# A six-block decoder on one core: projections and normalisations fused by chunks, expert choice inside the expert loop, head attention in fours

## The chip, the core and the metric

One core of a Trainium2 chip runs the whole program. TensorE (PE, its weight loads PEld) multiplies, VectorE (DVE), ScalarE (ACT) and GpSimd (POOL) work on vectors, SyncE (SP) issues DMAs; each runs its own queue in order, and they wait for each other's semaphores. The metric is the device time in microseconds (us), the median of three executions.

## The reference

`x` holds 32 sequences of 56 tokens with 128 features (1792 tokens); the context holds 32 × 1500 × 128 numbers. Every block is "add to x what a sublayer makes of the layer-normalised x":

```python
x = x + retention(norm(x))                 # 16 heads of 8, decay, rms, silu gate, Wo
x = x + context_attention(norm(x), ctx)    # one head, softmax over 1500 keys, Wv
x = x + experts0(norm(x))                  # 8 experts of 512, top 2, relu(g) * u
x = x + causal_attention(norm(x))          # 16 heads, rotary, wo
x = x + head_attention(norm(x), ctx)       # 16 heads of 8 over 1500 keys, Wo, bo
x = x + experts1(norm(x))                  # 8 experts, top 2 with a capacity,
                                           # silu, + 0.1 * a shared expert
# top 2: p = softmax(logits); one-hot of the best and the second best;
# weights p1, p2 divided by their sum; experts1 also counts, by a running sum over
# tokens, who still fits an expert's capacity, and drops the others
```

## The kernel before

The stream `xt` lies transposed in SBUF, 128 features by 1792 tokens, and is worked in `CH` = 4 chunks of `CW` = 448. Each stage is one or more blocks of hand-written queues for the five engines; at a block's end all engines meet. Semaphores are wrapped in `Flow` objects, and `rolled` and `staged` repeat a slot in hardware loops.

Between two stages stand separate blocks. `project_back` multiplies the sublayer's output by its last matrix and adds it to `xt`. `normalize` centres each chunk by a matmul, squares it on ACT, averages by a matmul, takes `Ln` and `Exp`, and multiplies on DVE into `xn`. The next stage's first projections are a block again. The chain of a chunk crosses PE, ACT and DVE.

`choose` is one more block before each expert stage. PE makes 14 tiles of 128 × 8 logits; ACT copies `xh` (`xn` rounded to a shorter float) while POOL subtracts to get the remainder `xl` and rounds the first expert's weights (`ahead.high`, `ahead.low`). DVE finds best and second best in a chain of small steps (with `capacity`, also the running counts of both ranks, one after the other). PE transposes the weights in 14 small transposes, ACT copies them, a DMA writes them to DRAM. Every expert then reads its row of weights back, spread over 128 partitions, into `cb`.

`experts_relu` (experts0) and `experts_silu` (experts1) run units of one chunk by 128 hidden features, 16 to an expert. PE multiplies the unit up in pieces (high × high, low × high, high × low), ACT applies the activation, POOL rounds the hidden values (`hf` to `hh`), DVE subtracts (`hl`), and PE multiplies down some units later. `weigh` (DVE) multiplies a finished chunk by `cb` into `ow`, which is then added to `xt`: on POOL in experts0, on DVE in experts1. In experts1 nine experts run, the shared one last.

`head_attention` works in slots, each with three samples in flight: the keys of sample p, the maxima (`peak`, 21 matmuls with a DVE maximum over each) and values (`values`) of p−1, and the scores, exponentials and weighted values of p−2 over 12 tiles of 125 keys (`score`, ACT `Exp`, `weigh`). A slot has six parts:

```python
    IT = ST // 2
    PLACES = [(0, 1, 2, 3), (1, 2, 3), (0, 1, 2, 3), (1, 2, 3), (0, 1, 2, 3), (0, 1, 2)]
                        if sums and i >= 1:
                            weigh(p - 2, u, 2 * i - 2)
                            weigh(p - 2, u, 2 * i - 1)
```

After the last slot the projection runs in the same block, and then `normalize` as "n6".

## Time and profile before

| what | us |
|---|---|
| median of 3 executions (lowest, highest) | 1730.73 (1729.13, 1732.51) |
| the profiled execution, its own time | 1733.57 |
| its span, first to last instruction | 1731.8 |

| stretch of the profiled execution | us |
|---|---|
| begin, retention, to the first context score | 0 to 137.4 |
| context attention | 137.4 to 292.9 |
| projection, n3, choose | 292.9 to 331.2 |
| experts0 | 331.2 to 573.95 |
| n4, rotary, causal attention | 573.95 to 699.1 |
| projection, n5, prologue of head attention | 699.1 to 729.1 |
| head attention's slots | 729.1 to 1480 |
| projection, n6, choose | 1480 to 1531.9 |
| experts1 and the output | 1531.9 to 1731.8 |

PE is busy 1575.7 us of the span (91%), DVE 1179.3 (68%), ACT 877.7 (51%), POOL 656.6 (38%); the mean granted clock of TensorE is 0.952 of full speed. A busy share is a mean over all stages; the windows of a single stage tell what bounds it.

### The profile page before, as it was taken

The page shows a single profiled execution, that of the slowest core. Times are in us where ns is not written, and L with a number is a line of the kernel's source. Part 1 is how long each engine was busy: PE and PEld are TensorE (multiplying, and loading weights), DVE is VectorE, ACT ScalarE, POOL GpSimd, SP SyncE. Part 2 cuts the span into 40 slices and gives each one's busy share as a digit, 9 for nine tenths or more (in the row PEclk, how much of TensorE's full clock was granted, in tenths as well). Part 3 has the DMA queues.
Part 4 walks back from the last instruction along what each step waited for, and adds up shares of the span by engine and source line. Part 5 has one row for each costly group of instructions (what it writes and reads, how often), then busy time and mean ns, then how long its engine had stood idle before and what let it go on. Part 6 is the DMA issues. An engine that isn't in the chain of part 4 may idle for free. (4 is left out here: it accounts for less than half of the span.)

```text
span 1731.8 us, 45100 instructions
## 1 busy us (share of the span) xinstructions
PE 1575.7 (91%) x16384; PEld 1202.0 (69%) x16384; DVE 1179.3 (68%) x1863; ACT 877.7 (51%) x1337; POOL 656.6 (38%) x717
## 2 busy tenths in 40 slices
PE   7988998699999866689999999999999999759998
PEld 3535665599999555367777777777777777448887
DVE  3643554487887567567777777777777776359998
ACT  4463332232322345356666666666666666334443
POOL 0300000387877245232333333323333331138886
PEclk8998999699999979899999999999999999769999
DMA  2028991311110000366665555556655554022221
GB/s 72 1 56 227 258 263 53 99 40 53 66 39 22 0 2 1 89 156 143 143 142 132 127 128 127 127 139 142 142 135 126 128 128 88 13 69 68 67 67 43
DMA packets 53038, 169.76 MB, mean 98 GB/s; under 512 B 12593, under 2 KB 24497, under 8 KB 52962
## 3 DMA queue, kind: packets, MB, share of 16 engines
q1 hardware_dynamic: 50802, 157.22, 36.2%
q10 hardware_dynamic: 2160, 11.52, 2.2%
q8 instruction: 48, 0.79, 0.2%
q14 instruction: 28, 0.23, 0.0%
HBM read 91.18 MB, written 1.04 MB: 53 GB/s over the span
## 5 line engine op out<-in xcount | busy, mean ns | idle before, releaser
L1728 DVE TENSOR_REDUCE hat_tops<-banks 128x1 f32<-128x500 f32 x672 | 448.3, 677 | 138.9 <-PE banks L1524 138.7
L1632 ACT ACTIVATE hat_pb<-banks 125x896 f32<-125x896 f32 x384 | 331.3, 916 | 149.6 <-PE banks L1543 148.3
L1524 PE MATMUL banks<-hat_kh,hat_qm 128*128 128x500 f32 x672 | 312.9, 467 | 3.9 <-DVE hat_tops L1728 3.5
L1677 POOL TENSOR_TENSOR hat_kl<-hat_kf,hat_kh 128x500 fp32r<-128x500 f32 x96 | 121.0, 1262 | 476.1 <-DMA hat_k<-hat_kh 303.3
L1543 PEld LDWEIGHTS banks<-hat_q,hat_k 128*125 128x125 f32 x1536 | 219.9, 189 | 42.9 <-issue 27.8
L1543 PE MATMUL banks<-hat_q,hat_k 128*125 128x224 f32 x1536 | 237.2, 278 | 8.8 <-issue 4.4
L1534 PEld LDWEIGHTS banks<-hat_pb,hat_vs 125*27 125x27 f32 (+1 forms) x6144 | 135.9, 98 | 72.6 <-ACT hat_pb L1632 38.9
L1534 PE MATMUL banks<-hat_pb,hat_vs 125*27 125x168 f32 (+1 forms) x6144 | 186.2, 262 | 0.1
L1524 PEld LDWEIGHTS banks<-hat_kh,hat_qm 128*128 128x128 f32 x672 | 128.7, 192 | 48.6 <-DVE hat_tops L1728 31.3
L1131 ACT ACTIVATE ffn_rg<-banks 128x448 f32<-128x448 f32 x128 | 69.7, 545 | 169.0 <-PE banks L1090 169.0
L1830 POOL CAST moe_hh<-moe_hf 128x448 fp32r<-128x448 f32 x144 | 116.8, 830 | 63.3 <-ACT moe_hf L1889 63.1
L1889 ACT ACTIVATE moe_hf<-banks,moe_b 128x448 f32<-128x448 f32 x144 | 91.1, 635 | 96.9 <-PE banks L1849 84.9
L1902 DVE TENSOR_TENSOR moe_hl<-moe_hf,moe_hh 128x448 fp32r<-128x448 f32 x144 | 127.1, 931 | 16.3 <-POOL moe_hh L1830 15.9
L1067 POOL CAST ffn_hh<-ffn_hf 128x448 fp32r<-128x448 f32 x128 | 104.0, 812 | 74.4 <-DVE ffn_hf L1156 73.6
L1156 DVE TENSOR_TENSOR ffn_hf<-ffn_rg,banks 128x448 f32<-128x448 f32 x128 | 79.0, 617 | 54.6 <-ACT ffn_rg L1131 52.7
L1143 DVE TENSOR_TENSOR ffn_hl<-ffn_hf,ffn_hh 128x448 fp32r<-128x448 f32 x128 | 103.6, 810 | 4.8 <-POOL ffn_hh L1067 4.8
L1553 PEld LDWEIGHTS banks<-w_HWvT,hat_ct 128*125 128x125 f32 x768 | 100.4, 190 | 4.1
L1564 PE MATMUL banks<-hat_ct,w_HWkT 128*128 128x500 f32 x192 | 99.9, 602 | 3.0 <-ACT hat_kf L1649 3.0
L1553 PE MATMUL banks<-w_HWvT,hat_ct 128*125 128x128 f32 x768 | 100.7, 275 | 0.0
L1088 PE MATMUL banks<-ffn_xh,ffn_wh 128*128 128x448 f32 x256 | 95.7, 374 | 3.9 <-DVEq L109 3.1
L1089 PE MATMUL banks<-ffn_xh,ffn_wl 128*128 128x448 f32 x256 | 94.7, 370 | 0.0
L1090 PE MATMUL banks<-ffn_xl,ffn_wh 128*128 128x448 f32 x256 | 94.5, 369 | 0.0
(290 smaller groups left out, 2907.1 us busy)
## 6 DMA issues: line engine op xcount, KB each, us to landing
hat_k<-hat_kh SPq DMA_DIRECT2D x256, 187.5 KB, 4.8
hat_ct<-ctxT SPq DMA_DIRECT2D x32, 750.0 KB, 6.2
hat_k<-hat_kl SPq DMA_DIRECT2D x128, 187.5 KB, 4.5
ctx_cx<-ctx SPq DMA_DIRECT2D x32, 672.0 KB
ctx_cd<-ctxT ACTq DMA_DIRECT2D x15, 750.0 KB, 5.4
moe_cb<-all_expert_weights SPq DMA_DIRECT2D x9, 896.0 KB, 4.7
ffn_cb<-all_expert_weights SPq DMA_DIRECT2D x8, 896.0 KB, 4.9
moe_raw<-Mw SPq DMA_DIRECT2D x18, 256.0 KB, 4.9
```

Source lines behind the costliest of these rows:

```text
L1067: high.inc(nc.gpsimd.tensor_copy(hh[:, j % 4, :], hf[:, j % 4, :]))
L1143: low.inc(v.tensor_tensor(hl[:, j % 4, :], hf[:, j % 4, :], hh[:, j % 4, :].bitcast(F32), ALU.subtract))
L1524: peak_out.inc(nc.tensor.matmul(g.bank(PK + m % 2)[:, 0:SB], qm[u][:].rearrange("p h i -> p (h i)")[:, r * 128:r * 128 + 128], kh[u][:, c ...
L1534: mm = nc.tensor.matmul(g.bank(PV)[32 * j:32 * j + V9 * w, n * L:(n + w) * L], vs[u][:, t, HG * j + n:HG * j + n + w, :].rearrange("p h e ...
L1543: mm = nc.tensor.matmul(g.bank(2 * (t % 2) + j // 2)[0:SW, (j % 2) * QW:(j % 2 + 1) * QW], k3[u][:, j, t * SW:(t + 1) * SW], q3[u][:, j, : ...
L1553: mm = nc.tensor.matmul(g.bank(MISC)[0:SW, (i % 4) * D:(i % 4 + 1) * D], ct[u][:, i * SW:(i + 1) * SW], g.w["HWvT"][:], start=True, stop=True)
L1564: k_out.inc(nc.tensor.matmul(g.bank(MISC)[:, 0:SB], g.w["HWkT"][:], ct[u][:, n * SB:(n + 1) * SB], start=True, stop=True))
L1632: exped.inc(nc.scalar.activation(pb[t % 4][:].rearrange("p (n i) -> p n i", n=2), g.ps[0:SW, 2 * (t % 2):2 * (t % 2) + 2, 0:2 * QW], ACT.E ...
L1677: k_low.inc(nc.gpsimd.tensor_tensor(kl[:, cols], kf[:, cols], kh[u][:, cols].bitcast(F32), ALU.subtract))
L1728: peaked.inc(v.tensor_reduce(tops[:, r, n:n + 1], g.bank(PK + m % 2)[:, 0:SB], AX_X, ALU.max))
L1830: high.inc(nc.gpsimd.tensor_copy(hh[:, j % 8, :], hf[:, j % 8, :]))
L1902: low.inc(v.tensor_tensor(hl[:, j % 8, :], hf[:, j % 8, :], hh[:, j % 8, :].bitcast(F32), ALU.subtract))
```

## The change

Six parts. (1) `normalize` and `project_back` become a class `Normal`, whose pieces stand inside the next stage's block: the projection of a chunk, its addition to `xt`, the norm and the next projection run chunk by chunk. (2) `choose` becomes a class `Choice`: its pieces stand between the units of the first expert; both ranks are counted in one pass and one transpose takes the place of 14. In experts1 the shared expert runs first with `cb` set to 0.1. (3) In the first expert of both stages ACT rounds `hh` and POOL subtracts `hl`. (4) In the other experts of experts1 POOL rounds the even units and ACT the odd ones, and `xt` is added on POOL. (5) Causal attention's rotary addition goes from DVE to POOL. (6) Head attention has three parts to a slot, weighs four tiles at a time, has six buffers `pb` instead of four, rounds keys on POOL, takes a reciprocal as `Ln` and `Exp` on ACT, and its output projection runs in the next block.

```diff
-def normalize(g, tag, spare=None, sync=None, gpsimd=None, vector=None):
+class Normal:
+    def on_pe(self, pe, then=None):
...
+        if self.project:
             for c in range(CH):
+                for n, (weight, source) in enumerate(self.project):
+                    mm = nc.tensor.matmul(g.bank(4 + c)[:, 0:CW], weight, chunk(source, c), start=(n == 0), stop=(n == len(self.project) - 1))
+                mm.then_inc(self.projected, 1)
+        for c in range(CH):
+            if self.project:
+                pe.wait_ge(self.added, c + 1)
+            nc.tensor.matmul(g.bank(c)[:, 0:CW], g.c["centre"], chunk(g.xt, c), start=True, stop=True).then_inc(self.centred, 1)
+            if c >= 1:
+                variance(c - 1)
+        after(0)
+        variance(CH - 1)
+        for c in range(1, CH):
+            after(c)
```

```diff
# experts_relu, TensorE and VectorE of expert 0
+                        if not later(e):
+                            if f == 0:
+                                pe.wait_ge(norm.x_low, c + 1)
+                            if j == 0:
+                                pe.wait_ge(norm.logged, CH)
+                            if 1 <= j <= 3:
+                                pe.wait_ge(norm.normed, (2, 2, CH)[j - 1])
+                                pick.on_pe_logits(g.bank(1), (0, 3, 7)[j - 1], (3, 7, TT)[j - 1])
...
+                            if j == TURN:
+                                pick.on_pe_turn(pe, g.bank(3))
...
-                        if j >= 1:
+                        if not later(e):
+                            choose(j)
+                            if j in (1, 5, 9):
+                                norm.parts(dve, (j + 3) // FT)
+                        elif j >= 1:
                             remainder(e, j - 1)
...
+                    if not later(e):
+                        for c in range(CH - 1):
+                            weigh(e, u, h, c)
```

```diff
# experts_silu, GpSimd and ScalarE
+                def add(e, c):
+                    weighted.wait(pool, e, c + 1)
+                    added.inc(nc.gpsimd.tensor_tensor(chunk(g.xt, c), chunk(g.xt, c), ow[:], ALU.add))
...
                     for j in range(UN):
-                        made.wait(pool, e, j + 1)
-                        down_out.wait(pool, *back(e, j, 8))
-                        pool.sem_inc(rounding, 1)
-                        high.inc(nc.gpsimd.tensor_copy(hh[:, j % 8, :], hf[:, j % 8, :]))
+                        if not later(e):
+                            remainder(e, j)
+                        elif j % 2 == 0:
...
+                            high_even.inc(nc.gpsimd.tensor_copy(hh[:, j % 8, :], hf[:, j % 8, :]))
+                        if j % FT == 2 and (j >= 10 or later(e)):
+                            add(*((e, (j - 10) // FT) if j >= 10 else (e - 1, (j + UN - 10) // FT)))
...
+                        if j >= 1 and (j % 2 == 0 or not later(e)):
+                            round_up(e, j - 1)
...
-                    weighted.wait(dve, e, c + 1)
-                    added.inc(v.tensor_tensor(chunk(g.xt, c), chunk(g.xt, c), ow[:], ALU.add))
```

```diff
# head_attention
-    IT = ST // 2
-    PLACES = [(0, 1, 2, 3), (1, 2, 3), (0, 1, 2, 3), (1, 2, 3), (0, 1, 2, 3), (0, 1, 2)]
+    IT = ST // 4
+    PLACES = [(0, 1, 2, 3, 5, 6, 7, 8), (0, 1, 2, 3, 4, 5, 6, 7), (0, 1, 2, 3, 4)]
-        pb = [sb(f"pb{k}", [SW, H * L]) for k in range(4)]
+        pb = [sb(f"pb{k}", [SW, H * L]) for k in range(6)]
...
                         if sums and i >= 1:
-                            weigh(p - 2, u, 2 * i - 2)
-                            weigh(p - 2, u, 2 * i - 1)
+                            for t in range(4 * i - 4, 4 * i):
+                                weigh(p - 2, u, t)
```

On TensorE, in a head slot whose maxima and sums both run (`hat_kh,hat_qm` is a peak, `hat_q,hat_k` a score of one key tile, `hat_pb,hat_vs` the weighing of half a tile), before:

```order
L1543 MATMUL banks<-hat_q,hat_k 125x224 x4
L1524 MATMUL banks<-hat_kh,hat_qm 128x500 x2
L1534 MATMUL banks<-hat_pb,hat_vs 27x168 x4
L1534 MATMUL banks<-hat_pb,hat_vs 9x56 x4
L1534 MATMUL banks<-hat_pb,hat_vs 27x168 x4
L1534 MATMUL banks<-hat_pb,hat_vs 9x56 x4
L1524 MATMUL banks<-hat_kh,hat_qm 128x500
L1543 MATMUL banks<-hat_q,hat_k 125x224 x4
```

and of the change:

```order
L1604 MATMUL banks<-hat_kh,hat_qm 128x500 x3
L1614 MATMUL banks<-hat_pb,hat_vs 27x168 x4
L1614 MATMUL banks<-hat_pb,hat_vs 9x56 x4
L1614 MATMUL banks<-hat_pb,hat_vs 27x168 x4
L1614 MATMUL banks<-hat_pb,hat_vs 9x56 x4
L1614 MATMUL banks<-hat_pb,hat_vs 27x168 x4
L1614 MATMUL banks<-hat_pb,hat_vs 9x56 x4
L1614 MATMUL banks<-hat_pb,hat_vs 27x168 x4
L1614 MATMUL banks<-hat_pb,hat_vs 9x56 x4
L1688 MATMUL banks<-constants,hat_top 7x128
```

Twice as many tiles are weighed in one run, and a slot changes to that kind of work and back three times where it did six times.

On GpSimd, in a late expert of experts1 (`moe_hh` is a rounding of hidden values, `moe_wh` and `moe_wl` are the next expert's weights), before:

```order
L1830 CAST moe_hh<-moe_hf 128x448 x6
L891 CAST moe_wh<-moe_raw 128x512
L1830 CAST moe_hh<-moe_hf 128x448
L895 TENSOR_TENSOR moe_wl<-moe_raw,moe_wh 128x512
L1830 CAST moe_hh<-moe_hf 128x448
L891 CAST moe_wh<-moe_raw 128x512
L1830 CAST moe_hh<-moe_hf 128x448
L895 TENSOR_TENSOR moe_wl<-moe_raw,moe_wh 128x512
L1830 CAST moe_hh<-moe_hf 128x448 x7
```

and of the change:

```order
L1982 CAST moe_hh<-moe_hf 128x448 x2
L1967 TENSOR_TENSOR xt<-xt,moe_ow 128x448
L1982 CAST moe_hh<-moe_hf 128x448
L894 CAST moe_wh<-moe_raw 128x512
L1982 CAST moe_hh<-moe_hf 128x448
L1967 TENSOR_TENSOR xt<-xt,moe_ow 128x448
L898 TENSOR_TENSOR moe_wl<-moe_raw,moe_wh 128x512
L894 CAST moe_wh<-moe_raw 128x512
L1982 CAST moe_hh<-moe_hf 128x448
L898 TENSOR_TENSOR moe_wl<-moe_raw,moe_wh 128x512
L1982 CAST moe_hh<-moe_hf 128x448
L1967 TENSOR_TENSOR xt<-xt,moe_ow 128x448
```

Half of the roundings have left the queue, and four additions to `xt`, which wait for DVE, have come in between.

On VectorE, where experts0 begins, the last steps of choosing and the first units before:

```order
L1011 TENSOR_REDUCE top_row<-top_w 128x14
L1013 TENSOR_SCALAR top_row<-top_row 128x14
L1016 RECIPROCAL top_row<-top_row 128x14
L1017 TENSOR_TENSOR top_w<-top_w,top_row 128x112
L912 UNCONDITIONAL_BRANCH
L1135 UNCONDITIONAL_BRANCH
L1156 TENSOR_TENSOR ffn_hf<-ffn_rg,banks 128x448 x2
L1143 TENSOR_TENSOR ffn_hl<-ffn_hf,ffn_hh 128x448
L1156 TENSOR_TENSOR ffn_hf<-ffn_rg,banks 128x448
```

and of the change, right behind the norm:

```order
L1232 TENSOR_TENSOR ffn_hf<-ffn_rg,banks 128x448 x2
L255 CAST n_xh<-xn 128x448
L257 TENSOR_TENSOR n_xl<-xn,n_xh 128x448
L1232 TENSOR_TENSOR ffn_hf<-ffn_rg,banks 128x448 x2
L957 COPY top_logits<-banks 128x112
L959 TENSOR_REDUCE top_row<-top_logits 128x14
L960 TENSOR_TENSOR top_tmp<-top_logits,top_row 128x112
L1232 TENSOR_TENSOR ffn_hf<-ffn_rg,banks 128x448
L969 TENSOR_REDUCE top_row<-top_sc 128x14
L970 RECIPROCAL top_row<-top_row 128x14
L971 TENSOR_TENSOR top_sc<-top_sc,top_row 128x112
```

The steps of choosing now stand between the products `ffn_hf` of the first expert.

## Rows read from the trace of the kernel before

**Rows 1.** Windows of the span: length, busy us (instructions) of each engine, clock, DMA.

```profile
292.90:331.20 38.30, 20.69 (x66) 12.62 (x66) 13.56 (x33) 11.88 (x22) 10.00 (x10) 0.67 0.08 23
...
361.80:539.35 177.55, 176.81 (x865) 161.49 (x865) 142.58 (x216) 52.32 (x97) 138.05 (x157) 1.00 0.16 54
...
774.73:1443.50 668.77, 662.33 (x8616) 507.42 (x8614) 495.08 (x813) 456.67 (x609) 217.02 (x232) 1.00 0.57 132
...
1531.86:1556.90 25.04, 20.39 (x82) 18.06 (x83) 15.46 (x16) 11.10 (x17) 15.83 (x19) 0.81 0.33 116
1577.80:1703.03 125.23, 120.16 (x578) 106.74 (x577) 118.97 (x146) 60.97 (x96) 103.66 (x121) 1.00 0.20 65
```

**Rows 2.** Timeline (start, us, engine, line, idle before): context attention's end to experts0.

```profile
292.94 3.25 PE L608 MATMUL banks<-ctx_zt,w_XWv 128*128 128x448 f32 x8 [0.85 <-PEq L688]
...
298.38 2.64 PE L199 MATMUL banks<-xt,constants 128*128 128x448 f32 x4 [2.20 <-PEq L2012]
...
306.90 0.63 ACT L217 ACTIVATE n_sd<-banks,eps_ln 128x448 f32<-128x448 f32 x1
...
309.29 6.08 PE L916 MATMUL banks<-w_FWrT,xn 128*128 128x8 f32 x28 [2.43 <-PEq L180]
...
309.90 4.40 POOL L934 TENSOR_TENSOR ffn_xl<-xn,ffn_xh 128x448 fp32r<-128x448 f32 x4 [214.58 <-ACT ffn_xh L943]
...
315.41 0.28 DVE L969 TENSOR_REDUCE top_row<-banks 128x14 f32<-128x112 f32 x1 [6.61 <-PE banks L916]
...
324.61 0.27 DVE L1017 TENSOR_TENSOR top_w<-top_w,top_row 128x112 f32<-128x112 f32 x1
```

**Rows 3.** Timeline of experts0: POOL's addition beside DVE's remainder.

```profile
454.13 1.16 POOL L1060 TENSOR_TENSOR xt<-xt,ffn_ow 128x448 f32<-128x448 f32 x1
...
454.95 0.82 DVE L1143 TENSOR_TENSOR ffn_hl<-ffn_hf,ffn_hh 128x448 fp32r<-128x448 f32 x1
```

**Rows 4.** Timeline of TensorE in one head slot.

```profile
916.10 0.47 PE L1524 MATMUL banks<-hat_kh,hat_qm 128*128 128x500 f32 x1
916.51 0.97 PE L1534 MATMUL banks<-hat_pb,hat_vs 125*27 125x168 f32 x32
917.41 0.69 PE L1543 MATMUL banks<-hat_q,hat_k 128*125 128x224 f32 x4
917.94 0.40 PE L1524 MATMUL banks<-hat_kh,hat_qm 128*128 128x500 f32 x1
918.17 0.59 PE L1543 MATMUL banks<-hat_q,hat_k 128*125 128x224 f32 x4
918.60 0.40 PE L1524 MATMUL banks<-hat_kh,hat_qm 128*128 128x500 f32 x1
```

**Rows 5.** Groups by line (busy us, mean ns, idle before) over the head slots.

```profile
L1632 ACT ACTIVATE hat_pb<-banks 125x896 f32<-125x896 f32 x348 | 300.2, 916 | 130.9 <-PE banks L1543 129.7
```

**Rows 6.** Timeline, from the end of head attention to experts1.

```profile
1478.06 2.03 PE L1534 MATMUL banks<-hat_pb,hat_vs 125*27 125x168 f32 x64
...
1481.53 6.24 PE L1615 MATMUL banks<-hat_ot,w_HWo 128*128 128x448 f32 x16
...
1490.15 3.16 PE L199 MATMUL banks<-xt,constants 128*128 128x448 f32 x4 [2.38 <-PEq L2012]
```

**Rows 7.** Groups by line, 1578 to 1700 us, in experts1.

```profile
L1902 DVE TENSOR_TENSOR moe_hl<-moe_hf,moe_hh 128x448 fp32r<-128x448 f32 x94 | 83.3, 934 | 5.4 <-POOL moe_hh L1830 5.4
L1830 POOL CAST moe_hh<-moe_hf 128x448 fp32r<-128x448 f32 x93 | 76.2, 837 | 21.6 <-ACT moe_hf L1889 21.6
...
L1912 DVE TENSOR_TENSOR xt<-xt,moe_ow 128x448 f32<-128x448 f32 x23 | 20.7, 902 | 0.8
...
L895 POOL TENSOR_TENSOR moe_wl<-moe_raw,moe_wh 128x512 fp32r<-128x512 f32 x12 | 15.5, 1288 | 0.0
```

**Rows 8.** Instructions of tiles moe_hl and moe_hh (ns shortest/median/longest).

```profile
L1902 DVE TENSOR_TENSOR moe_hl<-moe_hf,moe_hh x144: 609/973/1708, 1541.1 to 1724.0; 128x448 fp32r<-128x448 f32 x144
L1830 POOL CAST moe_hh<-moe_hf x144: 555/945/1042, 1540.5 to 1722.8; 128x448 fp32r<-128x448 f32 x144
```

More of the change, by code:

```diff
@@ L1242, in _ @@
             def _(dve):
+                norm.on_dve(dve)
                 n = 0
@@ L1608, in _ @@
[L1608 removed]
+                for t in range(ST - 4, ST):
+                    weigh(B - 1, 1, t)
+                sum_weights(B - 2)
                 sum_weights(B - 1)
[L1611 to L1616 removed]
@@ L1819, in _ @@
-                rolled(sp, N, slot)
+                        weighted.wait(sp, e - 2)
+                        sp.dma_start(cb[u][:], spread(g.ct_dram[e - 1], 0, 128)).then_inc(weights[u], 16)
+                        if not (isinstance(e, int) and e == N - 1):
+                            weighted.wait(sp, e - 1)
+                            sp.dma_start(b1[1 - u][:], g.d["Mb1"][e + 1]).then_inc(biases[1 - u], 16)
+                    else:
+                        pick.on_sp_keep(sp)
+                for e in range(2):
+                    ahead.load(sp, e, e)
+                    sp.dma_start(b1[e][:], g.d["Mb1"][e]).then_inc(biases[e], 16)
```

856 lines of the change are left out of this document (495 added, 361 removed).

## The prediction

> **What bounds the kernel now.** I read the windows first, stage by stage, then the timelines of the junctions between stages, then the groups by line where an engine is nearly full.
>
> In experts0 past its first expert PE is busy 176.81 of 177.55 us: six experts of 29.59, 144 matmuls each, .2055 us a matmul. In the head's regular slots it is busy 662.33 of 668.77; 29 slots, 23.06 each. In six experts of experts1 PE is busy 120.16 of 125.23, 20.87 an expert, and DVE 118.97: there the vector side is the limit, since 96 matmuls at .2055 would take 19.73. At a junction nothing is full: PE 20.69 of 38.30 us, at a clock of 0.67, between 2.4 and 1.2 GHz [rows 1]. So the junctions are chains of latencies, the head slots are PE's own sequence, and experts1 is a pair of vector engines.
>
> Durations come from the profiled execution, whose own time is 1733.57 (span 1731.8 and 1.8 around it). Its time is 2.84 above the median of the runs, 1730.73. I sum savings against 1733.57 and take the 2.84 off at the end. A measurement of this kernel tells about 0.2% (3.5 us) from no change.
>
> **Junction to experts0: +25 us at its first matmul, −9 inside the first experts, net +16.** Projection starts at 292.94, its chunks are out by 296.2; the norm's first matmul comes at 298.38, after 2.20 us idle at the block's end. Fused, that matmul follows the projections at 296.2. From it to the end of the last Ln took 306.90 + .63 − 298.38 = 9.15; the change lets the first unit start then (`norm.logged`), so 305.35, and I add .9 because additions and the first xh, xl stand on the same DVE. That gives 306.2 where it was 331.2: 25.0. The choosing chain (logits 309.29 to 315.4, DVE 315.41 to 324.88, then transposes and copies) leaves the path [rows 1, 2].
> Its work must then fit in expert 0. PE takes 28 logits: 6.08 at half clock, some 3 at full; the three weighings at the expert's end wait for the weights' DMA, some 2 (an estimate). So at least 5. The other end: DVE gets 9.5 us of choosing and three xh, xl pairs, in batches of some 1.5 between the products `ffn_hf`; a unit has 9 × .2055 = 1.85. A batch and a product (.6) are 2.1 already, and a subtraction on POOL takes 4.40 / 4 = 1.10 (the row of `ffn_xl`) [rows 2]. POOL's addition of 1.16 beside a DVE subtraction stretched that to .82, where .61 is its length alone [rows 3, 8]. If DVE waits out one of POOL's 1.10 in each of the seven batches, a unit takes 3.2, 1.4 too long: 10 in expert 0, and 2 of catching up. Range 5 to 12; I take 9, since both engines are nearly always occupied there.
>
> **Other fused junctions: +1.8 and +4.7.** Retention to context attention loses one block's end but its queries and keys wait for a DMA-fed first tile anyway: +1. In front of the rotary block one block's end goes: +.8. Into the head: the 2.20 idle goes, and queries start chunk by chunk; from the last Ln (307.53) to the first matmul of the next block (309.29) are 1.8 now, and the queries of three chunks move under the norm: 6 in all, by these rows. The bias matmul now comes first and PE waits for its addition, −1.3. Net +4.7, 2 to 8 [rows 2].
>
> **Head slots: +14.5.** A weighing block costs PE its transitions: from a peak to a weighing .41 against .23 to a score; a score after it lasts .53 to the next instruction, not .43. That is .28 a block, and three blocks a slot go: .84 [rows 4]. Against it: ACT must now give four exponentials of .916 in one part, among key and value copies, where PE asks for two scores close together (score and two peaks, .43 + .23 + .23 = .9) [rows 4, 5]. A score needs the exponential two tiles back; where a copy of some .6 stands between, PE waits. I see two such places a slot (scores 1 and 9), together 0 to .8. I take .34: a gain of .50 a slot, × 29 = 14.5. Without these waits, and with the slot's present idle (6.4 / 29 = .22 [rows 1]) gone too, 1.06 × 29 = 31; with .84 lost, 0. The key rounding on POOL, Ln and Exp for the reciprocal, and one slot's delay of sums are hidden: ACT is busy 456.67 / 29 = 15.7 and POOL 217.02 / 29 = 7.5 of 23 [rows 1]; uncovered they would cost their length, about 2 us a slot.
>
> **Head to experts1: +28.5 at the first matmul, −4.8 in expert 0.** Now the last weighing ends at 1480.1, projections run 1481.53 to 1487.8, the norm begins at 1490.15 [rows 6]. Changed: the last slot ends .9 later (four tiles in one block); sums, Ln, Exp and division all precede the projections (1.4 to the first of them now, some 4.8 then); then a block's end with semaphores cleared, 1.6 (an estimate; the ends seen cost 2.20 and 2.38 with an addition in them): 1487.4. Projections 6.24, more since part falls at half clock: norm at 1495.4, 5 later than now. Then 8.0 to the last Ln (9.15 less the part of ACT's table load that moves ahead, an estimate), so the first matmul at 1503.4 and not 1531.9: +28.5. Expert 0 takes 25.04 now, with a wait for its weights [rows 1]; the shared expert needs none, but has the choosing (9.5 us and the capacity's counts, about as much again) on DVE and 16 subtractions of 1.10 on POOL. Bounds 24.4 (all overlapped) to 32; I take 29.8, −4.8.
>
> **Experts1 past expert 0: −5, −1.5, −1.2.** Now an expert has on DVE 16 subtractions and 4 additions, on POOL 16 roundings and the next weights; the pair is the limit. Alone the subtraction takes .609 and the rounding .555; the medians are .973 and .945 [rows 8]: each stretches the other. The change moves 8 roundings to ACT, which is idle half the time (60.97 of 125.23 [rows 1]), and 4 additions (.902 now [rows 7], 1.16 on POOL [rows 3]) from DVE to POOL. Lower end: PE bounds, 19.73. Upper end: the two engines exclude each other wholly: 16 × .609 + 8 × .555 + 4 × 1.10 + 2 × 1.29 + 2 roundings of weights at .6 = 22.4. The same sum for the kernel before, 16 × .609 + 4 × .61 + 16 × .555 + 2 × 1.29 + 1.2, gives 24.8, where the trace has 20.87: they exclude each other in part only. POOL's addition waits for DVE's `weigh`, and roundings that PE needs queue behind it and behind the weights, so I take 21.5, .6 longer than now: 8 × .63 = −5. Expert 1 has the change of order, −1.5; at the end POOL's additions (1.16) take the place of DVE's: −1.2.
> The Trainium skill, "SBUF — State Buffer", section "SBUF: two separate sides", says that a GpSimd instruction and a VectorE instruction with two SBUF inputs hold a shared port pair exclusively, each for its whole length. By that rule the expert takes the 22.4 of the upper end; the trace agrees that they stretch each other (.973 against .609), and not on the whole length (20.87 against 24.8).
>
> **Sum.** 1.8 + 16 + 4.7 + 14.5 + 28.5 − 4.8 − 5 − 1.5 − 1.2 = 53.0. 1733.57 − 53.0 = 1680.6; less 2.84: 1678.
>
> **The rivals.**
> A. Vector engines keep up: experts1 is bound by PE (8 × (20.87 − 19.73) = +9, where I had −5) and the head's waits vanish half (+8). 1678 − 22 = 1656. For it: POOL's load per expert falls by 8 × .555 and rises by 4 × 1.16, so hardly grows, and DVE's falls. Against: the order, POOL behind DVE behind POOL.
> B. Fours buy nothing: exponentials bunched behind copies cost .84 a slot: 1678 + 14.5 = 1692; with the first experts at their long end (3 and 2), 1697. For it: ACT is busy two thirds and its order is fixed.
> C. Exclusion: POOL and DVE block each other wholly wherever work was moved to POOL. 22.4 an expert (7 more), the first experts at 12 and 32 (3 + 2), rotary 1: 1678 + 13 = 1691. For it: .973 against .609. Against: 20.87 against 24.8. The page of the Trainium skill named above would have it so.
> D. Slower than before: the weighing in fours holds `pb` and scores back so that ACT's twelve exponentials come in series with PE's blocks. A slot has to lengthen by 53 / 29 = 1.83 over my 22.56, to 24.4, to cancel all the rest; from there on the kernel is slower. At two exponentials and a half exposed in every slot it is 1678 + 29 × 2.3 = 1745. Against: six buffers, four in use, and ACT a third idle.
> E. The junctions don't overlap, since the first expert waits for the choosing (its `cb`, 112 × 128 numbers by DMA) at its end: both lose up to 10 more. 1698.
>
> **How the numbers follow.** My forecast .42, A .2, B .15, C .1, E .08, D .03, and .02 for a change that the measurement can't tell. Likeliest 1678; its own range 1664 to 1692. All but 2 in 10: from 1651 (A with 5 more from the head) to 1703 (E or B with 5 more). Faster .95, same .02, slower .03.
>
> **What would show it.** In the changed profile: first matmul of experts0 13 us behind the projection's start (38.3 now) and of experts1 23 us after the last weighing; expert 0 of experts0 some 36 and of experts1 about 30; head slots 22.5; experts of experts1 at 21.5, with POOL's `xt` additions at 1.16 or longer. Wrong I would be if slots stay at 23 or fall under 22, if an expert of experts1 takes 19.8, or if the first experts run at 31, as if nothing had been put in.

## The result and the profile after

The changed kernel takes 1683.49 us (median of 4 executions, 1680.12 to 1688.33), against 1731.51 for the kernel before on the same chip (4 executions): a ratio of 0.9727, with a 95% interval of 0.97 to 0.9753. It is faster by 2.7%, inside the predicted range and 5.5 us above the predicted 1678. The profiled execution took 1683.96, 49.6 less than the profiled one of before (1733.57). Of the experiments' executions one, a second of experiment 1, took 2167.79 us at a mean granted clock of .645; it is left out below.

The head of the page: TensorE's busy time fell by 31 us, so more than half of the gain is busy time of PE, not idle time.

```profile
span 1682.2 us, 45110 instructions
...
PE 1544.6 (92%) x16354; PEld 1198.6 (71%) x16354; DVE 1129.9 (67%) x1760; ACT 881.1 (52%) x1387; POOL 726.3 (43%) x786
```

Windows of the profile after, with the columns of [rows 1]: projection to the first unit of experts0, its experts 0, 1, and 2 to 7; projection to the first peak of head attention, two first slots, 29 regular slots; last weighing to the first unit of experts1, its expert 0, and experts 2 to 7.

```profile
296.61:307.43 10.82, 9.68 (x24) 4.31 (x25) 6.51 (x9) 7.11 (x13) 5.20 (x6) 1.00 0.48 148
307.43:344.14 36.71, 32.07 (x164) 28.30 (x165) 25.06 (x48) 16.10 (x33) 22.54 (x21) 1.00 0.12 40
344.14:376.37 32.23, 29.81 (x146) 26.81 (x144) 24.95 (x37) 9.75 (x19) 25.32 (x28) 1.00 0.33 117
376.37:553.89 177.52, 176.89 (x867) 161.88 (x866) 140.42 (x217) 52.58 (x97) 132.25 (x151) 1.00 0.11 40
689.52:711.11 21.59, 17.57 (x39) 7.68 (x39) 11.85 (x19) 10.09 (x18) 13.13 (x6) 0.89 0.25 77
711.11:760.29 49.18, 40.04 (x285) 28.50 (x283) 31.25 (x47) 17.60 (x24) 21.49 (x25) 0.79 0.77 173
760.29:1409.15 648.86, 638.60 (x8611) 506.94 (x8610) 488.86 (x782) 425.27 (x579) 270.19 (x319) 1.00 0.59 136
1447.09:1469.54 22.45, 16.71 (x41) 8.00 (x41) 6.80 (x14) 8.40 (x17) 8.93 (x9) 0.85 0.23 71
1469.54:1498.78 29.24, 24.09 (x115) 21.66 (x116) 22.72 (x51) 18.37 (x34) 14.91 (x13) 0.84 0.00 1
1521.35:1650.83 129.48, 120.37 (x578) 109.88 (x576) 104.30 (x121) 82.86 (x145) 95.62 (x97) 0.97 0.20 64
```

Read against [rows 1], the same stretches give the ledger of the 49.6 us:

| stretch | before | after | gain | forecast |
|---|---|---|---|---|
| start to context attention's projection | 292.9 | 296.6 | −3.7 | +1 |
| projection to the first unit of experts0 | 38.3 | 10.8 | +27.5 | +25 |
| experts 0 and 1 of experts0 | 60.2 | 68.9 | −8.8 | −9 |
| experts 2 to 7 | 177.5 | 177.5 | 0 | 0 |
| end of experts0, n4, rotary, causal attention, to its projection | 130.2 | 135.6 | −5.4 | +.8 |
| that projection to the first peak | 30.0 | 21.6 | +8.4 | +4.7 |
| first two head slots | 45.6 | 49.2 | −3.6 | 0 |
| 29 regular slots | 668.8 | 648.9 | +19.9 | +14.5 |
| last slot and way to experts1 | 88.4 | 60.4 | +28.0 | +28.5 |
| experts1: expert 0; 1; 2 to 7 | 25.0; 20.9; 125.2 | 29.2; 22.6; 129.5 | −4.2; −1.7; −4.2 | −4.8; −5 for eight experts and −1.5 for expert 1 |
| last expert and output | 28.8 | 31.4 | −2.6 | −1.2 |

The gains add to 49.6. The fused junction shows in the timeline of experts0's start (before it, [rows 2]): projection, the first centring 3.1 us behind it instead of 5.4, the last chunk's Ln at 306.65, and the first unit .8 later.

```profile
296.61 3.25 PE L204 MATMUL banks<-xn,w_XWv 128*128 128x448 f32 x8 [2.09 <-PEq L2215]
...
299.70 1.67 PE L209 MATMUL banks<-xt,constants 128*128 128x448 f32 x4
...
306.65 0.64 ACT L230 ACTIVATE spare<-banks,eps_ln 128x448 f32<-128x448 f32 x1
```

In experts0's two first experts the list of waits names what PE idles for (us in total, times, longest): above all the product `ffn_hf` on DVE.

```profile
PE banks L1118 <- DVE ffn_hf L1232: 5.7, 4, 2.3
PE banks L935 <- DVE top_by_expert L1028: 1.2, 1, 1.2
PE banks L1118 <- ACT spare L230: 0.8, 1, 0.8
```

In six late experts of experts1 (groups by line, answering [rows 7]) the rounding is shared by POOL and ACT, DVE has lost its additions, and yet each subtraction lasts longer (995 ns, 934 before); POOL's addition lasts 1465:

```profile
L2091 DVE TENSOR_TENSOR moe_hl<-moe_hf,moe_hh 128x448 fp32r<-128x448 f32 x97 | 93.4, 995 | 25.2 <-POOL moe_hh L1982 20.6 <-PE banks L2008 3.2 <-ACT moe_hh L2061 1.1
...
L1982 POOL CAST moe_hh<-moe_hf 128x448 fp32r<-128x448 f32 x49 | 39.4, 815 | 0.9 <-ACT moe_hf L2068 0.8
...
L2006 PE MATMUL banks<-moe_hh,moe_wh 128*128 128x448 f32 x96 | 36.3, 378 | 9.1 <-DVE moe_hl L2091 9.1
...
L1967 POOL TENSOR_TENSOR xt<-xt,moe_ow 128x448 f32<-128x448 f32 x24 | 35.2, 1465 | 33.0 <-DVE moe_ow L2099 33.0
```

### The profile page after: what moved, and what is told of

Same layout as the page of the kernel before. It is cut to its first block and busy times, and to the rows that moved or that the text cites. A ratio compares the mean times of both kernels' runs of the same rounds, so it can differ in the third digit from the quotient of the medians.

```text
span 1682.2 us, 45110 instructions
## 1 busy us (share of the span) xinstructions
PE 1544.6 (92%) x16354; PEld 1198.6 (71%) x16354; DVE 1129.9 (67%) x1760; ACT 881.1 (52%) x1387; POOL 726.3 (43%) x786
## 5 line engine op out<-in xcount | busy, mean ns | idle before, releaser
L1728 ACT ACTIVATE hat_pb<-banks 125x896 f32<-125x896 f32 x384 | 340.2, 916 | 226.0 <-PE banks L1623 221.6
L1604 PE MATMUL banks<-hat_kh,hat_qm 128*128 128x500 f32 x672 | 299.4, 463 | 8.2 <-issue 4.8
L1623 PE MATMUL banks<-hat_q,hat_k 128*125 128x224 f32 x1536 | 250.9, 286 | 12.8 <-ACT hat_pb L1728 9.2
L1799 POOL CAST hat_kh<-hat_kf 128x500 fp32r<-128x500 f32 x96 | 58.6, 610 | 391.5 <-DMA hat_k<-hat_kh 303.6
L1614 PE MATMUL banks<-hat_pb,hat_vs 125*27 125x168 f32 (+1 forms) x6144 | 166.9, 261 | 0.1
L1091 POOL CAST ffn_hh<-ffn_hf 128x448 fp32r<-128x448 f32 x112 | 91.1, 813 | 51.4 <-DVE ffn_hf L1232 51.4
L894 POOL CAST ffn_wh<-ffn_raw 128x512 fp32r<-128x512 f32 x24 | 15.4, 641 | 203.9 <-DMA ffn_raw<-FWdT 203.9
L1118 PE MATMUL banks<-n_xh,ffn_wh 128*128 128x448 f32 x256 | 95.0, 371 | 7.3 <-DVE ffn_hf L1232 5.7
L1203 DVE TENSOR_TENSOR ffn_hl<-ffn_hf,ffn_hh 128x448 fp32r<-128x448 f32 x113 | 92.2, 816 | 4.2 <-POOL ffn_hh L1091 4.2
L1120 PE MATMUL banks<-n_xl,ffn_wh 128*128 128x448 f32 x256 | 93.6, 366 | 0.0
```

The lines of the kernel that those rows point to most:

```text
L1118: nc.tensor.matmul(out, a_high, b_high, start=start, stop=False, skip_group_check=True)
L1120: return nc.tensor.matmul(out, a_high, b_low, start=False, stop=stop, skip_group_check=True)
L1203: low.inc(v.tensor_tensor(hl[:, j % 4, :], hf[:, j % 4, :], hh[:, j % 4, :].bitcast(F32), ALU.subtract))
L1604: peak_out.inc(nc.tensor.matmul(g.bank(PK + m % 2)[:, 0:SB], qm[u][:].rearrange("p h i -> p (h i)")[:, r * 128:r * 128 + 128], kh[u][:, c ...
L1614: mm = nc.tensor.matmul(g.bank(PV)[32 * j:32 * j + V9 * w, n * L:(n + w) * L], vs[u][:, t, HG * j + n:HG * j + n + w, :].rearrange("p h e ...
L1623: mm = nc.tensor.matmul(g.bank(2 * (t % 2) + j // 2)[0:SW, (j % 2) * QW:(j % 2 + 1) * QW], k3[u][:, j, t * SW:(t + 1) * SW], q3[u][:, j, : ...
```

## Experiments

Every edit stands against the changed kernel, unless it says otherwise; times are medians, ratios are to the kernel before, timed beside each experiment. Where an interval is given and it overlaps the change's (0.97 to 0.9753), the whole times can't be told apart, and the reading rests on the stage alone.

**1. Weighing blocks (h_split).** A part's four tiles in two blocks with a peak between, that is six blocks a slot again and everything else of the change kept.

```diff
                         top(3)
+                        if sums and i >= 1:
+                            for t in range(4 * i - 4, 4 * i - 2):
+                                weigh(p - 2, u, t)
...
                         top(4)
                         if sums and i >= 1:
-                            for t in range(4 * i - 4, 4 * i):
+                            for t in range(4 * i - 2, 4 * i):
                                 weigh(p - 2, u, t)
```

> The changed kernel, but a slot weighs its four tiles two and two, with one peak between (two transitions more per block, six blocks a slot again). If the change of work on TensorE is what fours saved, a regular slot goes from 22.39 to 22.39 + 3 x .28 = 23.2 us, and the kernel is 29 x .84 = 24 us slower than the changed one (about 1708). The rival says that fours save little by themselves and that the slot got shorter by its other edits (key rounding on GpSimd, six buffers, fewer ACT steps): then the slot stays within .2 of 22.39 and the kernel within 6 us of 1683.5.

28 regular slots:

```profile
777.16:1429.70 652.54, 640.30 (x8319) 492.75 (x8317) 478.43 (x756) 411.25 (x561) 261.09 (x308) 1.00 0.56 131
```

A slot takes 23.31, against 22.39 in the same 28 slots of the change. Of the .91 more, .83 are PE's busy time (22.87 against 22.04) and .08 idle: .28 of busy time for each of three more blocks. The theory of the transitions stands. The whole execution took 1704.56, where 1708 was expected.

**2. An exponential ahead of a key copy (h_swap).** If a copy in front of exponential 4i+3 makes score 1 wait, exchanging the two frees it.

```diff
+                        if sums and i >= 1:
+                            exponential(p - 2, 4 * i + 3)
                         if i >= 1 and keys:
                             copy_keys(p, 2 * i - 2)
-                        if sums:
+                        if sums and i == 0:
                             exponential(p - 2, 4 * i + 3)
```

> The changed kernel, but in parts 1 and 2 of a slot ACT computes the fourth exponential ahead of the key copy and not behind it. In the changed trace TensorE waits .24 of idle (.40 longer from issue to issue) ahead of score 1 and .11 (.275) ahead of score 9, and each of these scores needs an exponential that stands behind a key copy. If that is their cause, both waits go and a slot falls from 22.39 to about 21.7 (29 x .67 = 19 us, about 1664). The rival: the key copy comes .9 later, so that TensorE waits for it at the next key or value instead, and the slot stays within .2 of 22.39.

It is 26 us worse: 1709.52, ratio 0.9848 (0.9806 to 0.989), a slot of 23.40. The wait at score 1 shrank by .14 only. A new wait of .96 for a maximum appeared; the timeline of one slot shows its origin:

```profile
947.35 2.11 POOL L1787 TENSOR_TENSOR hat_q<-hat_qs,constants 96x224 fp32r<-96x224 f32 x4
947.53 2.07 DVE L1838 TENSOR_TENSOR spare<-hat_on,hat_rc 128x112 f32 x1 [0.44 <-ACT hat_rc L1723]
...
950.98 0.49 PE L1604 MATMUL banks<-hat_kh,hat_qm 128*128 128x500 f32 x1 [0.96 <-DVE hat_tops L1855]
```

DVE's product with the reciprocal, .28 when POOL is quiet, met POOL's train of four placements and lasted as long as the train: 2.07 (the median of its 32; 1.10 in the change). The two maxima behind it came late, and PE waited for them. What I took for a question of ACT's order is one of which DVE instruction meets which POOL instruction.

**3. That product moved away from the train (h_swap_div, against h_swap).**

```diff
-                                if m == 4 and reached(p, 4):
+                                if m == 8 and reached(p, 4):
                                     divide(p - 4)
-                                if m == 4 and reached(p, 3):
+                                if m == 8 and reached(p, 3):
                                     pick(p - 3)
```

> The kernel with the fourth exponential ahead of the key copy (23.40 a slot), and VectorE's division and picking moved from peak 4 to peak 8 of a slot. In that kernel's trace the division, a multiplication of two SBUF tensors, took 2.07 us and not .28: it waited behind GpSimd's four placements of q (.56 each), and TensorE then waited .9 to .97 for a maximum in every slot. If that blocking is the whole loss, the slot falls to 22.3 (the .14 that the swap gave at score 1 is then seen, against 22.39 in the changed kernel). The rival: the loss has to do with the later key copy itself (maxima and values waiting for keys), and the slot stays at 23.4.

The slot falls to 22.68, the time to 1688.32 (0.9744, 0.9702 to 0.9786): .72 of the 1.02 gone by moving two DVE steps, and the product is back at a median of .28. It shows that the meeting was most of the cost. It still isn't better than the change as made: PE's idle time is the change's again (.34 a slot against .35), but its busy time is .30 a slot more (22.34 against 22.04), and where that comes from I haven't separated. The order of copies and exponentials in the change is as good as any tried.

**4. Experts1 with the additions back on DVE (m_dve).** The roundings stay shared between POOL and ACT.

```diff
-                        if j % FT == 2 and (j >= 10 or later(e)):
-                            add(*((e, (j - 10) // FT) if j >= 10 else (e - 1, (j + UN - 10) // FT)))
...
+                    weighted.wait(dve, e, c + 1)
+                    added.inc(v.tensor_tensor(chunk(g.xt, c), chunk(g.xt, c), ow[:], ALU.add))
...
```

> The changed kernel, but in experts1 the addition to xt is made by VectorE again; the roundings stay shared between ACT and GpSimd. My theory: in the changed trace each of the four GpSimd additions (1.46) runs beside a subtraction that lasts 1.57 and not .61, so it costs VectorE about 1 us each where the addition itself would cost it .6 to .9; with them back an expert takes 19.9 to 20.3 in place of 21.58, bound by TensorE, and the kernel gains about 9 us (1674). The rival: VectorE becomes the bound again, 16 x .61 + 4 x .67 + 4 x .9 = 16 and what waits in between, 20.9 an expert as before the change: a gain of 5 or less. A third: the two engines exclude each other by a whole instruction, whoever adds, and nothing moves.

Expert 0, then experts 2 to 7, and the two groups that answer to those above:

```profile
1464.45:1496.51 32.06, 24.04 (x114) 21.64 (x115) 26.83 (x53) 18.32 (x34) 16.19 (x14) 0.81 0.00 1
1516.34:1631.54 115.20, 115.20 (x577) 107.98 (x576) 106.89 (x145) 82.79 (x145) 66.33 (x73) 1.00 0.22 72
```

```profile
L2082 DVE TENSOR_TENSOR moe_hl<-moe_hf,moe_hh 128x448 fp32r<-128x448 f32 x97 | 78.1, 851 | 7.5 <-ACT moe_hh L2052 7.3
L1978 POOL CAST moe_hh<-moe_hf 128x448 fp32r<-128x448 f32 x49 | 36.8, 750 | 50.7 <-ACT moe_hf L2059 50.7
...
L2093 DVE TENSOR_TENSOR xt<-xt,moe_ow 128x448 f32<-128x448 f32 x24 | 17.3, 722 | 0.8
```

19.20 an expert, PE busy without a gap; 1661.17 in all, ratio 0.9579 (0.9538 to 0.962). DVE has more to do than in the change (106.89 against 104.30 us), POOL much less (66.33 against 95.62), and PE never waits. So DVE's load was not the limit; POOL's additions were. How they cost is seen in the change, ahead of one of PE's six waits:

```profile
1576.85 2.10 DVE L2091 TENSOR_TENSOR moe_hl<-moe_hf,moe_hh 128x448 fp32r<-128x448 f32 x2
...
1577.00 1.46 POOL L1967 TENSOR_TENSOR xt<-xt,moe_ow 128x448 f32<-128x448 f32 x1 [1.15 <-DVE moe_ow L2099]
...
1578.42 1.68 POOL L898 TENSOR_TENSOR moe_wl<-moe_raw,moe_wh 128x512 fp32r<-128x512 f32 x1
...
1580.04 0.61 POOL L894 CAST moe_wh<-moe_raw 128x512 fp32r<-128x512 f32 x1
...
1580.60 0.56 POOL L1982 CAST moe_hh<-moe_hf 128x448 fp32r<-128x448 f32 x1
...
1581.12 1.26 POOL L898 TENSOR_TENSOR moe_wl<-moe_raw,moe_wh 128x512 fp32r<-128x512 f32 x1
...
1581.29 2.47 DVE L2091 TENSOR_TENSOR moe_hl<-moe_hf,moe_hh 128x448 fp32r<-128x448 f32 x2 [2.35 <-POOL moe_hh L1982]
...
1583.01 0.44 PE L2006 MATMUL banks<-moe_hh,moe_wh 128*128 128x448 f32 x1 [1.95 <-DVE moe_hl L2091]
```

Two things come together. The engines meet: POOL's addition starts while the first of two subtractions runs; together the two take 2.10, where two of .61 would take 1.2, and the second ends at 1578.95, .5 behind POOL's addition (1577.00 + 1.46). No matmul waits for these two. And POOL's queue is long: behind the addition, which had waited 1.15 for `moe_ow`, stand a remainder and a rounding of weights, then the rounding that DVE needs. DVE is idle for 2.35 until that rounding is done, then its subtraction meets POOL once more (1.57 where it takes .61 alone), and the matmul waits 1.95. Over the six experts DVE waits 20.6 us for roundings on POOL and PE 9.1 us for DVE (four times 1.95 and twice .65, all of PE's idle time there). Which part is the queue's and which the meetings' no run separates, since both go with the additions.

**5. POOL's next weights spread over the expert (m_spread).** The rival to experiment 4: additions, roundings and weights heap up in units 5 to 9.

```diff
-                        if 5 <= j < 9 and later(e) and not (isinstance(e, int) and e == N - 1):
+                        if j in (5, 8, 11, 13) and later(e) and not (isinstance(e, int) and e == N - 1):
...
```

> The changed kernel, but in experts1 GpSimd makes the next expert's weights at units 5, 8, 11 and 13 and not at 5, 6, 7 and 8. In the changed trace the only waits of TensorE there (9.1 us in six experts, up to 2.0 each) come at unit 8 to 9 behind a subtraction, after GpSimd has made two weight roundings, two remainders of 1.3 to 1.7 and an addition in a row. If that heap is the cause, the waits go and an expert takes 20.1, as the ones without a wait do now: 7 x 1.45 = 10 us, about 1673. The rival: the pair of engines is simply full, and the waits move to other units with the same sum, 21.6 an expert.

```profile
1512.51:1641.11 128.60, 118.95 (x578) 106.63 (x576) 112.20 (x121) 82.89 (x145) 97.72 (x97) 1.00 0.22 71
```

21.43 an expert, against 21.58: the waits moved (12 of .8 now, 9.7 us in all), and where the weights stand is not the cause. The whole took 1675.74 (0.9679, 0.963 to 0.9728), which the intervals don't tell from the change; of the 8.1 us between the two profiled executions 7.3 lie ahead of experts1, in stages that the edit doesn't touch.

**6. Both ways back (m_dve_cast).** The additions of experts1 on DVE, in expert 0 too, and past expert 0 all 16 roundings on POOL, as before the change.

```diff
-                        elif j % 2 == 0:
+                        else:
                             made.wait(pool, e, j + 1)
...
+                            high[j % 2].inc(nc.gpsimd.tensor_copy(hh[:, j % 8, :], hf[:, j % 8, :]))
...
```

> The changed kernel, but past expert 0 of experts1 both moves are undone: VectorE adds to xt and GpSimd rounds all sixteen units. This is the kernel before's sharing and I expect its period, 20.9 an expert, against 19.20 with the additions on VectorE and half of the roundings on ACT, and 21.58 with both moves. Then the ACT share is worth 1.7 us an expert and the move of the additions costs 2.4. The rival: 19.2 here too, since the period before was set by something else (the weights' timing, the loading order).

```profile
1516.40:1641.16 124.76, 119.27 (x577) 106.39 (x576) 117.38 (x146) 61.13 (x96) 104.39 (x121) 1.00 0.21 67
```

20.79 an expert, as before the change (20.87); 1675.28 (0.9664, 0.9634 to 0.9693). The two halves of part 4 of the change, taken in this order, thus are worth: ACT's share of the roundings +1.6 an expert (20.79 to 19.20), the additions on POOL −2.4 (19.20 to 21.58). The fourth combination, additions on POOL and all roundings too, was not run.

**7. The two additions that fall into experts1's expert 0 on POOL, the rest on DVE (m_mix, beside m_dve).** In expert 0 DVE has the choosing, and expert 0 had grown by 2.8 in experiment 4.

```diff
+                        if j in (10, 14) and not later(e):
+                            add(e, (j - 10) // FT)
...
```

> The run before with VectorE's additions in experts1 (19.20 an expert, but 32.06 for expert 0 in place of 29.24, where TensorE waited 5.5 and not 2.6 us for the transpose) with one difference: the two additions that fall into expert 0 stay on GpSimd. VectorE is the engine that chooses there, so I expect expert 0 at 29.2 and the others at 19.2: 2.8 us less than that run's 1661. The rival: expert 0 was longer because its TensorE waits stand elsewhere by chance, and nothing is gained (within 1 us of 32).

Expert 0 takes 29.41 and expert 1 21.74, the others 19.20. The sum of the first two is 51.15, against 51.89 in m_dve: .7 won where 2.8 were expected, since expert 1 gave 1.9 back. The time, 1662.78 (0.9589, 0.9562 to 0.9616), can't be told from m_dve's.

**8. Experts0 without its two searches for the best (f_nochoice).** The weights are then the softmax over all eight experts; DVE has 16 small steps fewer.

```diff
-                    if j == 5:
-                        pick.best(dve, 0, pick.sc)
...
-                    if j == 7:
-                        pick.best(dve, 1, pick.rest)
                     if j == 8:
-                        pick.chosen(dve)
+                        pick.step(dve, v.tensor_copy(pick.w1[:], pick.sc[:]))
```

> The changed kernel, but in experts0 VectorE leaves out both searches for the best expert and what stands between them (16 small steps of units 5 to 8; the weights are the plain softmax over all eight experts). In the changed trace expert 0 of experts0 takes 36.71 us and expert 1 32.23, against 29.58 for the others. Alone these 16 steps take 4.3 us, and in the trace 7.4, some of them 1.0 to 1.26 beside a GpSimd subtraction where they take .27 alone. If the choosing in VectorE's queue is what lengthens the first expert, it falls by about 5 to 32, with the waits of 1.9 and 1.1 at units 7 to 9 gone. The rival: GpSimd's own chain of subtractions and weight roundings sets the pace of expert 0, and it stays within 1 us of 36.7.

```profile
304.05:337.58 33.53, 31.41 (x164) 28.46 (x165) 20.01 (x34) 15.86 (x33) 22.62 (x21) 1.00 0.13 40
```

Expert 0 falls from 36.71 to 33.53, but expert 1 rises from 32.23 to 33.74. A good part of DVE's queue taken away wins 1.7 of the 9.8 us that the two experts take above twice the 29.59 of a later one. The one execution took 1674.99; it tells nothing of the total.

**9. POOL's weights later in expert 0 (f_late).**

```diff
-                        if 5 <= j < 11 and not (isinstance(e, int) and e == E - 1):
+                        start = 5 if later(e) else 10
+                        if start <= j < start + 6 and not (isinstance(e, int) and e == E - 1):
...
```

> The changed kernel, but in expert 0 of experts0 GpSimd makes the next expert's weights (three roundings, three remainders of 1.3) at units 10 to 15 and not 5 to 10, so not beside the searches for the best. If the stretching of VectorE's steps beside GpSimd is what costs, expert 0 falls by 2 to 3 us from 36.7 and expert 1 stays at 32.2, since all weights are there in time. The rival: the sum of GpSimd's work is the same and the wait moves to units 10 to 15 or into expert 1; the two experts together stay within 1 us of 68.9.

35.68 and 34.93, in sum 1.7 more than in the change, though some .6 of that is this execution's pace (its later experts take 29.90 and not 29.59); 1685.77 (0.9729, 0.9688 to 0.977). The waits moved to expert 1, one of them for the weights:

```profile
PE banks L1119 <- DVE ffn_hf L1233: 4.9, 2, 3.3
PE banks L1119 <- POOL ffn_wl L898: 1.6, 1, 1.6
```

**10. The choosing ahead of the first unit (f_first).** The norm stays fused; only the interleaving of the choosing in experts0 is undone.

```diff
+                            if j == 0:
+                                pe.wait_ge(norm.normed, CH)
+                                pick.on_pe_logits(g.bank(1))
+                                pe.wait_ge(pick.ready, 1)
...
+                    if not later(e):
+                        for j in range(3, 10):
+                            choose(j)
```

> The changed kernel, but in experts0 the choosing stands ahead of the first unit again, as in the kernel before (logits, then VectorE's chain, and TensorE's first unit waits for it); norm, projections and all queues are otherwise as changed. This prices the interleaving alone. The first unit then comes at 306 + 3 to 6 for the logits + 10 for the chain, 12 to 16 later than in the changed kernel; expert 0 loses its waits at units 7 to 9 and the logits (36.7 to about 32). Net 8 to 11 us slower than the changed kernel. The rival: without small steps between the units expert 0 falls under 31 and expert 1 to 30, and the interleaving was worth less than 5 us.

```profile
293.66:320.11 26.45, 15.76 (x52) 10.30 (x52) 14.43 (x36) 7.86 (x14) 5.95 (x6) 0.73 0.19 60
320.11:351.55 31.44, 31.17 (x136) 27.62 (x137) 14.67 (x21) 15.22 (x31) 22.01 (x20) 0.90 0.16 51
```

The first unit comes 26.45 behind the projection (10.82 in the change), and experts 0 and 1 take 31.44 and 32.22, 5.3 less in sum. The interleaving is worth 15.6 − 5.3 = 10.3 us, of the 18.7 that the junction and its experts gained in all. The whole took 1689.98 (0.9749, 0.9724 to 0.9773), 6.5 more than the change where 8 to 11 were expected; its profiled execution was 3.0 ahead when the projection began. Expert 1 keeps its excess of 2.65 without any choosing in reach: it must have another cause.

**11. The kernel before, profiled again (before_again).** It measures what an execution varies by, stage by stage.

> The kernel before, profiled once more. Stages whose code the change leaves alone took other times in the profiles so far: retention's block from its first projection to the gate's 87.6 us before and 84.6 to 89.2 in six executions of changed kernels, the causal loop's weighings 73.3 before and 74.7 to 76.8. If that is the granted clock of each execution and not the change, this profile of the kernel before differs from its first by 1 to 3 us in these stages, and not in experts0 (29.58 an expert) or the head (23.06 a slot). The rival: the kernel before gives 87.6 and 73.3 again within .2, and the causal loop is really some 2 to 3 us longer after the change.

Two slots of causal attention in it, and two in the profile after:

```profile
630.73:635.87 5.14, 3.71 (x101) 2.84 (x93) 3.81 (x6) 3.58 (x10) 3.00 (x3) 0.83 0.01 3
635.87:640.56 4.69, 3.11 (x93) 2.30 (x94) 3.70 (x6) 2.87 (x7) 2.50 (x3) 1.00 0.00 0
```

```profile
618.47:624.07 5.60, 4.34 (x95) 3.58 (x96) 3.61 (x6) 2.78 (x7) 3.51 (x4) 0.70 0.02 4
624.07:628.67 4.60, 3.10 (x94) 2.30 (x96) 3.60 (x6) 2.77 (x7) 1.59 (x2) 1.00 0.01 4
```

The same kind of slot takes 4.60 at a granted clock of 1.00 (2.4 GHz) and 5.60 at 0.70, a mean between that level and 1.2 GHz. Both kernels have such slow slots: 4 in the first profile of before, 2 in this one, 4 to 6 in those of the changed kind that I counted. The whole loop of weighings took 73.3 and 72.8 in the two profiles of before, and 74.0 to 77.6 in the twelve of the changed kernel and its variants (76.8 in the change's own). The context loop took 140.3 to 141.3 in most profiles of both kernels and 145.7 to 147.0 in three, this one (146.8) among them. Retention, from its first projection to the gate's, took 84.6 to 89.2, and began at 16.1 to 17.7 us.

**12. A version made of what was found (best_c, against m_mix).** Own buffers for the first two weighed chunks of experts0's expert 0, so that its weighings needn't wait for POOL's additions, and no wait for the bias in n5.

```diff
-        ow = sb("ow", [128, CW])
+        ow, ows = sb("ow", [128, CW]), [sb(f"ow{k}", [128, CW]) for k in range(2)]
+        out_of = lambda e, c: ows[c] if isinstance(e, int) and e == 0 and c < 2 else ow
...
-                pe.wait_ge(biased, 1)
...
```

> The version with the additions of experts1 on VectorE past expert 0, and two small things more: in experts0 the first two weighed chunks of expert 0 have buffers of their own, so that VectorE need not wait for GpSimd's addition between the three weighings at the expert's end (in the changed trace they stretch from 344.9 to 349.7 and TensorE waits 2.3 in expert 1), and in the head's prologue TensorE doesn't wait for the bias (1.2). I expect expert 1 of experts0 at 30.2 and not 32.2, the projection after causal attention 1 earlier, and 3 us less than the 1661 to 1663 of the two runs with VectorE's additions: 1659. The rival: the wait moves to the next product and nothing but the bias is gained, 1661.

What it rests on is the start of expert 1 of experts0 in the change: three weighings into one buffer alternate with POOL's additions.

```profile
344.91 0.62 DVE L1210 TENSOR_TENSOR ffn_ow<-banks,ffn_cb 128x448 f32<-128x448 f32 x1
...
347.18 0.62 DVE L1210 TENSOR_TENSOR ffn_ow<-banks,ffn_cb 128x448 f32<-128x448 f32 x1 [1.65 <-POOL xt L1083]
...
349.11 0.62 DVE L1210 TENSOR_TENSOR ffn_ow<-banks,ffn_cb 128x448 f32<-128x448 f32 x1 [1.31 <-POOL xt L1083]
...
350.32 0.47 PE L1118 MATMUL banks<-n_xh,ffn_wh 128*128 128x448 f32 x1 [2.30 <-DVE ffn_hf L1232]
```

Expert 1 fell from 32.23 to 30.38, and experts 2 to 7 of experts1 stay at PE's floor (115.20 in all):

```profile
343.93:374.31 30.38, 29.82 (x146) 26.81 (x145) 24.87 (x37) 9.77 (x19) 25.38 (x28) 1.00 0.35 125
```

The wait for the bias gave back .4 and not the 1.2 expected: from the last causal matmul's end to the projection 3.1 us and not 3.5.

1657.4 us (1656.04 to 1663.3), ratio 0.9566 (0.9545 to 0.9587): faster than both kernels, by 26 us against the change. From m_mix (1662.78) and m_dve (1661.17) the intervals don't tell it; nearly all of the gain is that of the additions on DVE.

## Why the prediction was right, and where not

**Junctions.** Right in size, 27.5 for 25 and 28.0 for 28.5, and in mechanism as far as the timeline tells: the chain projection, norm, first unit ran as the rows of before said, and from the last weighing to experts1 it took 22.45 for the forecast 23. Experiment 10 tested the interleaving at the first junction (10.3 us). At the second, the largest gain of all, no experiment undid anything, nor was the fused norm undone at either.

**First experts.** In experts0 −8.8 for −9, but by my mechanism only in part, so this match is luck. I had 3 for the logits, 2 for the weighings, and the rest for seven batches of DVE steps, each held up by POOL's subtraction: up to 10 us in expert 0 and 2 after. Measured against twice 29.59, the two experts take 9.8 more: 2.5 more busy time of PE in expert 0 (logits and transposes), waits there of 3.4 for `ffn_hf` and 1.2 for the transpose's input, and 2.65 in expert 1, of which the alternation of weighing and addition gave back 1.85 when it was removed (shown by experiment 12). In the kernel before, expert 0 itself took 1.0 more than a later one. Experiment 8 took the two searches away and won 1.7 in all. What starts each of the waits for `ffn_hf` I haven't separated. In experts1 −4.2 for −4.8.

**Head slots.** The step on transitions held: predicted .84 a slot, measured .82 (PE busy 22.84 before, 22.02 after, and .28 a block in experiment 1). What I mis-sized is the term of the waits: I took .34 a slot, and PE's idle time rose only from .22 to .35, .13 more. Hence 19.9 and not 14.5. The waits stand where I put them, before score 1 (.24 at 895.50 in the timeline) and score 9 (.11):

```profile
895.50 0.70 PE L1623 MATMUL banks<-hat_q,hat_k 128*125 128x224 f32 x4 [0.24 <-ACT hat_pb L1728]
```

But "where a copy of some .6 stands between, PE waits" fell: with the copy out of the way .14 of the wait at score 1 went and none at score 9 (experiment 2). For the rest the profile names the exponential itself.

**Experts1.** −.71 an expert for −.6: close, and the reason given held: POOL's addition waits for DVE's `weigh`, and roundings that PE needs queue behind it and behind the weights (the rows of experiment 4 show just that). What failed is the floor: I took .2055 us a matmul from experts0 (19.73), and experts1 runs at .200 (115.20 / 576), 19.20. And rival A hung on loads, which did fall in the change (DVE 118.97 to 104.30, POOL 103.66 to 95.62 in six experts), while PE's waits grew: the order and the meetings decide, not the loads. With the additions on DVE, experts1 became what A said, and better. Rival C's whole exclusion, by the prediction's own sum, would give that sharing 16 × .609 + 8 × .555 + 4 × .61 + 2 × 1.29 + 1.2 = 20.4 an expert; it took 19.20. The engines stretch each other, but in part only.

**What I had at "+1" and "+.8".** This is the step that failed most: the stretch before context attention's projection lost 3.7, causal attention 5.4, and the first two head slots 3.6, 12.7 against +1.8 forecast. Fusing moved the clearing of semaphores at the block's end ahead of the projection: 1.2 of the 3.7 (12.2 to 13.4 from the last of the context loop's matmuls to it, the same in all twelve profiles of the changed kind) and, with the bias and the wait for it, 2.3 of the 5.4 (1.2 to 3.5 from the last matmul's end to it), which the next stretches gave back. Most of the remainder lies in loops whose instructions hardly changed: 1.6 in retention's (87.6 before, 89.2 after, and 86.2 when the kernel before ran again), 3.5 in the causal weighings, and in the first two slots all 3.6, at a granted clock of .79 where it was .89. For retention and the first slots, repeated profiles spread as far as the difference (four variants had 45.2 to 46.2 for the two slots, as before had 45.6, and eight 48.1 to 49.3 with the change). For the causal weighings none of twelve profiles reached the two of before. Whether the change brings its slow slots, for instance by the rotary addition that went to POOL, stays open; it wasn't tried apart.

**The sum.** Misses of +2.5 and +3.7 at junctions, +5.4 in the slots and −14.5 in stages taken for untouched and −.5 in the rest make the sum 49.6 and not 53.0. The other 2.4 us are the step from one execution to the median: I took 2.84 off, and the changed kernel's profiled execution stands only .5 above its median. The parts were worse than the total, and that the total came so near is in part luck.

## What to carry to other kernels

A junction's chain can be priced from the timeline of the kernel before, to some 2 us. When an elementwise step with two SBUF inputs is moved from DVE to POOL, don't count its length alone but whom it meets and what then queues behind it: rounding went to ACT at a gain, the addition to POOL at a loss that ate it. And put the stages that a change seems not to touch into the range with their own spread, here 3 to 5 us each.

## What the hardware showed

A DVE instruction with two inputs from SBUF that meets a row of POOL instructions without gaps ends with the row, not with its first instruction (.28 alone, 2.07 beside four placements in 2.11, experiments 2 and 3). Small steps suffer as well as large ones; one of experts0's choosing, in the profile after:

```profile
322.38 1.16 POOL L1079 TENSOR_TENSOR ffn_hl<-ffn_hf,ffn_hh 128x448 fp32r<-128x448 f32 x1 [0.69 <-ACT ffn_hh L1175]
322.47 1.20 DVE L979 TENSOR_TENSOR top_hot<-top_tmp,top_row 128x112 f32<-128x112 f32 x1
```

A step of .27 alone lasts 1.20; another, beside POOL's 1.32, lasts 1.25. POOL stretches too: its addition takes 1.13 at the shortest and 1.15 by median in experts0, and 1.46 by median in experts1, where it starts while a subtraction of DVE runs. And the granted clock of causal attention's loop changes from slot to slot between 1.00 and .70, at 1.0 us for each slow slot, and how many there are differs between executions of one kernel (4 and 2 in the two of before).
